# Two attention layers rewritten: halves of the array for S and T, heads of 50 stacked rows, more work on GpSimd

## The reference: two layers over a stream of 32 x 256 x 256

```
x += attn0(ln(x), ctx)   16 heads of 16, q/k/v/o projections with low-rank terms
x += sqrt((ln(x) @ cos(..))^2 + (ln(x) @ sin(..))^2)
x += attn1(ln(x), ctx)   the same heads, rotary embedding on q and k
x += quantised feed-forward, 256 -> 1024 -> 256, gelu
attn: softmax(q k^T / 4) v per head, then the output projection
```

## Time and profile before

| | us |
|---|---|
| median of 3 runs | 2490.02 (2481.99 to 2492.55) |
| span of the profiled execution | 2491.9 |
| L496 in layer 0, first to last of 32 | 124.8 to 836.1 |
| L496 in layer 1, first to last of 32 | 1093.4 to 2079.1 |

### The profile page before, as it was taken

The page is one execution under the profiler, slowest core; times in us unless marked ns, Lnnn a source line. Parts: engine busy times, 40 slices in busy tenths (PEclk is TensorE's granted clock), DMA queues, the critical chain, the costliest instruction groups (busy, mean ns, idle before and its releaser), DMA issues. The chain is left out here.

```text
span 2491.9 us, 47293 instructions
## 1 busy us (share of the span) xinstructions
PE 1955.9 (78%) x14240; PEld 1576.1 (63%) x14240; DVE 1747.3 (70%) x3674; ACT 1316.8 (53%) x2381; POOL 797.0 (32%) x866
## 2 busy tenths in 40 slices
PE   1689999999999679277788777887777775786687
PEld 0567777777777467255666666666666663665676
DVE  6567778877877378465667767767666665676788
ACT  0255666656655378144444444444444443786676
POOL 3012222222222200423333333333333332221787
PEclk9899999999999689578888888888888877898899
DMA  5576887888878100356665656666666661356565
GB/s 164 107 157 145 169 172 162 166 169 166 170 161 165 53 3 0 76 104 122 123 120 116 117 109 116 119 112 118 111 118 122 121 118 54 135 220 252 196 242 186
DMA packets 259781, 333.54 MB, mean 134 GB/s; under 512 B 29152, under 2 KB 237184, under 8 KB 251520
## 3 DMA queue, kind: packets, MB, share of 16 engines
q1 hardware_dynamic: 233088, 277.00, 49.4%
q0 software_dynamic: 26624, 55.67, 9.6%
HBM read 185.70 MB, written 144.70 MB: 133 GB/s over the span
## 5 line engine op out<-in xcount | busy, mean ns | idle before, releaser
L610 DVE TENSOR_REDUCE L_negm<-L_s_bank 128x2 f32<-128x512 f32 x1024 | 684.4, 684 | 363.2 <-PE L_s_bank L418 360.7
L475 ACT ACTIVATE L_prob<-L_t_bank 128x512 f32<-128x512 f32 x1024 | 598.9, 598 | 631.8 <-PE L_t_bank L429 625.7
L418 PE MATMUL L_s_bank<-L_kst,L_qst 96*128 96x256 f32 x2048 | 526.1, 343 | 236.5 <-DMA L_kst<-k_scratch 176.7
L418 PEld LDWEIGHTS L_s_bank<-L_kst,L_qst 96*128 96x128 f32 x2048 | 355.4, 216 | 363.0 <-issue 142.0
L429 PE MATMUL L_t_bank<-L_qst,L_kst 98*128 98x256 f32 x2048 | 460.6, 311 | 18.3 <-ACT L_prob L475 15.2
L429 PEld LDWEIGHTS L_t_bank<-L_qst,L_kst 98*128 98x128 f32 x2048 | 361.7, 217 | 33.3 <-ACT L_prob L475 30.0
L339 PE MATMUL L_o_bank<-L_prob,L_vext 128*32 128x256 f32 x4096 | 301.1, 415 | 2.7 <-ACT L_prob L475 2.7
L1289 PE MATMUL G_acc<-G_w_out,G_hhl 128*128 128x256 f32 x1024 | 140.4, 291 | 59.4 <-DVE G_hhl L1259 59.1
L259 POOL DMA_DIRECT2D L_den<-o_scratch x64 | 35.5, 554 | 452.2 <-DMA o_scratch<-L_osb 452.2
L1289 PEld LDWEIGHTS G_acc<-G_w_out,G_hhl 128*128 128x128 f32 x1024 | 127.9, 192 | 72.1 <-DVE G_hhl L1259 37.5
L339 PEld LDWEIGHTS L_o_bank<-L_prob,L_vext 128*32 128x32 f32 x4096 | 112.5, 115 | 92.6 <-issue 18.8
(11 more groups left out here) (172 smaller groups left out, 3257.2 us busy)
## 6 DMA issues: line engine op xcount, KB each, us to landing
L_qst<-q_scratch SPq DMA_DIRECT2D x384, 128.0 KB, 5.0
L_kst<-k_scratch SPq DMA_DIRECT2D x384, 128.0 KB, 6.4
q_scratch<-L_qhl SPq DMA_DIRECT2D x64, 512.0 KB, 3.0
k_scratch<-L_khl SPq DMA_DIRECT2D x64, 512.0 KB, 3.2
o_scratch<-L_osb POOLq DMA_DIRECT2D x128, 256.0 KB, 4.8
hidden_scratch<-G_hid SPq DMA_DIRECT2D x32, 1024.0 KB, 3.9
G_hid<-hidden_scratch SPq DMA_DIRECT2D x32, 1024.0 KB, 7.4
L_ctx_in<-in_ctx SPq DMA_DIRECT2D x64, 256.0 KB, 3.2
```

The costliest lines, as they stand in the source:

```text
L418: mm = pe.matmul(s_bank[k % 2][:, j, :], qst[1 - q][0:96, h, P * qt:P * (qt + 1)], kst[1 - q][0:96, h, :], start=True, stop=True)
L475: act.activation(prob[g % 2][:, k % 2, 2 * (k // 2 % 2):2 * (k // 2 % 2) + 2, :], t_bank[k % 2][:, :, :], ACT.Exp, scale=HD ** -0.5).then_ ...
L610: dve.tensor_reduce(negm[:, t, 2 * pair:2 * pair + 2, qt], s_bank[k % 2][:, :, :], AX.X, ALU.max, negate=True).then_inc(sem["dve_s"], 1)
```

## The change

- Heads are regrouped: a step at one j takes head j of either 128-row tile. Of the 8 heads of a tile, 4 sit at partitions 0 to 49 of the stacks, 4 at 64 to 113 (48 rows and 2 for maximum and ones). For batch n and half h the partitions start at 64 * (n % 2 ^ h), so that S of batch i+1 and T of batch i, issued alternately (S, T, S, T), always lie in opposite halves.
- Stacks: 8 DMAs a batch of 2 KB runs in place of 12 of 1 KB runs; no zeroed rows.
- The pipeline is one batch longer (project q and k for batch i+3), all steps written out (no `Fori`). Output products `weighted` (two a batch, 16 matmuls each, in place of four of 8) write two banks `eo` that are copied at once.
- Order on TensorE: after k = 2 maxima's transpose, project v and `weighted(i-1, 1)`; after 4 the transposes (layer 1: and project k); after 6 project q; after 7 project k (layer 0); after 10 project o, maxima's transpose and `weighted(i, 0)`.
- ScalarE takes q and k with bias as float32, v's copy, `eo`; VectorE keeps reductions, low parts of x and ctx, maxima, reciprocal, residual sum, statistics. GpSimd takes the normalisation, the splits of q and k, the low part of y, the scaling, and in layer 1 the whole rotation, whose half swap is a DMA.
- v's bias is folded into the output bias. The reciprocals are spread by a broadcasting DMA (the mask matmul goes). All DMAs go to SyncE's queue. Layer 0 stores the split transposed ctx to DRAM, and layer 1 loads it (no transposes and splits of ctx there).

The diff, cut to its core: the stacks, SyncE's step (between what stands here it issues, in order: stores of k and q, 4 DMAs; the load of ctx; sums of the exponentials, 2; half swap of k, 2, or ctx store; merge of the outputs, 4; later reciprocals out, 2; half swap of q, 2; last, reciprocals back, 1) and TensorE's step:

```diff
-        qst = [sb(f"qst{j}", [98, H, S], F32R) for j in range(2)]
+        qst = [sb(f"qst{j}", [P, HJ, KT, S], F32R) for j in range(2)]
...
+            def stack(n, half):
+                u = n % 2 ^ half
+                for st, dram, high in ((kst[n % 2], k_dram[n % 2], KH), (qst[n % 2], q_dram[n % 2], QH)):
+                    part = dram.rearrange("(j d) c t q -> j d c (t q)", d=HD)[HJ * u:HJ * (u + 1)]
+                    sp.dma_start(st[64 * u:64 * u + 2 * HD, :, :, :].bitcast(F32), part.rearrange("j d c n -> (d c) j n")).then_inc(sem[f"stack{half}"], 16)
+                    sp.dma_start(st[64 * u + 2 * HD:64 * u + ROWS, :, :, :].bitcast(F32),
+                                 part[:, :, high, :].rearrange("j d n -> d j n")).then_inc(sem[f"stack{half}"], 16)
...
+            def step(i):
+                if on(i + 1):
+                    after(sp, sem["pe_t"], 16 * i)
+                    stack(i + 1, 1)
+                if on(i):
+                    maxima(i, 1)
...
+                    after(sp, sem["pe_t"], 16 * i + 8)
+                    stack(i + 2, 0)
...
+                if on(i + 1):
+                    maxima(i + 1, 0)
...
+                for k in range(16):
+                    first = scores(i + 1, k) if on(i + 1) else iter(())
+                    second = scores_T(i, k) if on(i) else iter(())
+                    for _ in range(KT):
+                        next(first, None)
+                        next(second, None)
+                    if k == 2:
+                        if on(i):
+                            after(pe, sem["dve_mT"], 2 * i + 1)
+                            maxima(i, 1)
+                        if on(i + 2):
...
+                            project_rows(m1, cT[(i + 2) % len(cT)], whl["v"]).then_inc(sem["pe_v"], 1)
+                        if on(i - 1):
+                            weighted(i - 1, 1)
+                    if k == 4 and on(n):
...
+                    if k == 6 and on(n):
...
+                    if k == 10:
+                        if on(i - 2):
+                            pe.wait_ge(sem["pool_yl"], i - 1)
+                            after(pe, sem["act_kf"], min(n + 1, hi))
...
+                            project_rows(m1, yhl, whl["o"]).then_inc(sem["pe_o"], 1)
+                        if on(i + 1):
+                            after(pe, sem["act_qf"], min(n + 1, hi))
+                            maxima(i + 1, 0)
+                        if on(i):
+                            weighted(i, 0)
```

More of the change, by code:

```diff
@@ L197, in stack @@
[L197 to L204, removed]
@@ L433, in _, with scores @@
-            drive(pe, step)
+            def scores(n, k):
+                half, j, qt = k // 8, k % 8 // 2, k % 2
+                u = n % 2 ^ half
+                if k % 8 == 0:
+                    pe.wait_ge(sem[f"stack{half}"], 64 * (n + 1))
+                after(pe, sem["dve_s"], 16 * n + k - 1)
+                rows = slice(64 * u, 64 * u + ROWS)
+                for t in range(KT):
+                    mm = pe.matmul(s_bank[k % 2][:, t, :], qst[n % 2][rows, j, t, P * qt:P * (qt + 1)], kst[n % 2][rows, j, t, :],
+                                   start=True, stop=True)
+                    if t == KT - 1:
+                        mm.then_inc(sem["pe_s"], 1)
+                    yield
@@ new lines, in scores_T @@
+            def scores_T(n, k):
+                half, j, kt = k // 8, k % 8 // 2, k % 2
+                u = n % 2 ^ half
+                if n == lo and k == 0:
+                    pe.wait_ge(sem["ones0"], 64)
+                if k % 8 == 0:
+                    pe.wait_ge(sem[f"m_load{half}"], 16 * (n + 1))
+                after(pe, sem["act_p"], 16 * n + k - 1)
+                rows = slice(64 * u, 64 * u + ROWS + 2)
+                for t in range(KT):
+                    mm = pe.matmul(t_bank[k % 2][:, t, :], kst[n % 2][rows, j, t, P * kt:P * (kt + 1)], qst[n % 2][rows, j, t, :],
+                                   start=True, stop=True)
+                    if t == KT - 1:
+                        mm.then_inc(sem["pe_t"], 1)
+                    yield
@@ L435, in _ @@
+            drive(step)
         @block.scalar
@@ L670, in start @@
+                    if k == 13 and on(i - 2):
+                        b = i - 2 - lo
+                        dve.wait_ge(sem["dve_bn"], i - 1)
+                        for t in range(NT):
+                            ins = dve.bn_aggr(stats[:, 2 * b + t, :], bst[:, t, :])
+                        ins.then_inc(sem["dve_st"], 1)
+            drive(step)
+            dve.wait_ge(sem["dve_st"], hi)
 def start(core, x, x_res, stats, consts, src):
```

793 lines of the change are left out of this document (351 added, 442 removed).

## The result

The changed kernel takes 2748.66 us (median of 4 runs, 2741.91 to 2750.83) where the kernel before, beside it, takes 2491.28 (2481.99 to 2502.78): a ratio of 1.1033, 95% interval 1.0982 to 1.1084. The prediction was 2467, range 2320 to 2580: wrong in sign and outside the range. The profiled execution has a span of 2747.7 us at a mean granted clock of 0.803 (before: 2491.9 at 0.880).

The account below looks back on a forecast made before the run. Before, TensorE bounds layer 0, waits bound layer 1. Steps: 24.4 + 0.3 + 2.0 = 26.7 and 24.75 + 0.5 + 2.0 = 27.25; span 2491.9 + 117.8 - 141.1 = 2468.6, median 2467 us, range 2320 to 2580.

Parts of the forecast that it names:

- Halves side by side: TensorE, S and T: pairs in opposite partition halves overlap, 0.24 us for one k instead of 0.48.
- Rival C: S and T: halves do not run side by side, 0.48 a k, about 1.0 us a step; 2529 us, chance 0.10.
- The schedule of layer 0 at full clock: Layer 0's step: six parts sum to 24.4 us against 22.9 before; GpSimd beside VectorE adds 0.3.
- part 1: Layer 0, k = 11 to 2 of the next step: VectorE sets the pace, 6.35 us.
- switches of the tiling mode: TensorE: a whole matmul of 0.28 at some ten switches, 1.3 us more a step, would give 2548 us.
- The clock: Both layers: TensorE's clock falls, costing 2.0 us a step on the path; bounds nothing and 3.3.
- rival B: Blocks after k = 2 and project q: clock falls every step, 3.5 us layer 0, 2.7 layer 1; 2557 us, chance 0.20.
- ScalarE's added waits and SyncE's queue: Moved work: ScalarE has about 3 us before T 3, SyncE is 13 us of 24 busy; cost nothing.
- D: SyncE's one queue: a wait holds the stacks, S 0 waits as before; 2.2 us a step, 2603 us, chance 0.07.
- The k stack's wait of before: Layer 1: S's wait for stacks, 120.7 us for k's in the window before, goes; step 24.75 against 31.8.
- GpSimd beside VectorE: VectorE's maxima splits wait while GpSimd is busy: 0.3 us a step in layer 0, 0.5 in layer 1.
- Big blocks and VectorE's work no longer lie beside each other: Layer 0: this gives back the gain from TensorE's work dropping to some 15.8 us; step 24.4 against 22.9.

Follow-up runs that it names:

- g3: The changed kernel with S and T of one k in the same half of the array; 2872.1 us, ratio 1.152 to the kernel before.
- i3: The changed kernel with k and q stores before the second maxima, and S and T of ten k's issued twice; 2596.0 us, ratio 1.038 to the kernel before.
- g2_stores: The changed kernel with SyncE's stores of k and q ahead of the second maxima's load; 2597.2 us, ratio 1.043 to the kernel before.
- g4_spread: The changed kernel with project v moved to k = 13 and output products issued in halves at k = 1, 2, 12, 14; 2435.0 us, ratio 0.977.
- g1: The changed kernel with S and T issued twice at k = 0, 1, 3, 4, 5, 11 to 15; 2692.7 us, ratio 1.081.
- h2: The changed kernel with only v's projection moved, from after k = 2 to after k = 13 of its own batch's step; 2589.4 us, ratio 1.036.
- i1_swap_early: The changed kernel with v late, products split, stores before second maxima, and q's half swap right behind k's in SyncE's order; 2336.2 us, ratio 0.939.

## Why the prediction was wrong, step by step

1. **Halves side by side: right.** 0.24 a k, as taken. Rival C is refuted by the trace, and its price was short by half: 62 us estimated, some 120 measured. Of g3's 3.0 us a step in layer 0, half of the added low is 2.8: the price came by way of the clock.
2. **The schedule of layer 0 at full clock: near.** 24.7 with GpSimd's share; some 24.8 by i3's step at full clock. There the blocks took 3.9, 5.0 and 3.6, forecast 3.9, 4.7 and 3.65. In the change itself part 1, k = 11 to 2, was 6.35 and measured 6.3; S 3 to project q 4.7 and 4.9; the wait for k's evacuation 1.1 and 1.2. The 1.3 us that the prediction named for switches of the tiling mode is not there: these blocks leave no room for it (and ten switches of 0.28 would have been 2.8).
3. **The clock: the step that failed in layer 0.** I took 2.0 us a step, from layer 1's mean clock of before and one fall there; it costs some 5.9. The block after k = 2 took 6.8 for 3.9, project q to S 10 6.4 for 4.7, the block after k = 10 5.1 for 3.65: 6.0 more in these three, of the 6.3 by which the sum of 24.4 fell short of 30.7. My upper bound of 3.3 was itself too low: it allowed one fall a step, in the first block and project q, and there are two, and they reach project k, project o and both sets of products as well. The mechanism was rival B's, at 1.7 times its price (3.5 against 5.9): B has 28.5 us for layer 0, measured 30.7. What I had weighed wrongly was a mean: a mean clock says nothing of which work meets the low stretches, and here it is the work that everything waits for. The Trainium skill (TensorE: Matmul & The Clock Gate, Terms) puts the penalty of throttled time at half of its length; the trace comes near, 13.7 / 2 = 6.8 against the 5.9 found by parts, and 5.2 between i3's two steps.
4. **ScalarE's wait for the store: the step that failed in layer 1.** I costed ScalarE's added waits and SyncE's queue at nothing and asked only whether the stacks would be late. They were not (S waits for no DMA in either window), so D is wrong as put; but the store of q stood behind the second maxima, and g2_stores gives 5.0 us a step for it in the middle of the layer, 4.8 over all 31 distances, of which some 2.0 came through the clock. The forecast went by all distances: 27.25 + 4.8 = 32.05, of the 33.05 measured. What makes the last 1.0 isn't shown. In all: layer 0 missed by 205.2 - 117.8 = 87.4 us, layer 1 by 39.0 + 141.1 = 180.1, the rest of the program by 11.6, together the 279.1 between 2747.7 and 2468.6. The forecast took a whole step for all 31 distances; that those at the ends are shorter (29.6 against 30.7 us on average in layer 0) made the miss smaller than its terms were off.
5. **The k stack's wait of before: right**, it is gone (120.7 us to none), and without the store's wait layer 1 comes in at 28.2 over all distances (g2_stores), for 27.25.
6. **GpSimd beside VectorE: small, as said.** The split of the maxima, which answers to the earlier trace rows, in layer 0 and then in layer 1:

```profile
L559 DVE CAST L_mhl<-L_negm 128x16 fp32r<-128x16 f32 x53 | 9.3, 175 | 1.8
```

```profile
L559 DVE CAST L_mhl<-L_negm 128x16 fp32r<-128x16 f32 x53 | 24.9, 470 | 1.8
```

In layer 1 the mean is 0.3 us more, twice a step, so 0.6 in all for the cast, of which half is on the path by the schedule; in layer 0 nothing. The forecast had 0.5 and 0.3.

7. **"Big blocks and VectorE's work no longer lie beside each other": seen, and its consequence missed.** It stood in the working as the reason for 24.4 over 22.9. g4_spread shows what it was worth: 6.4 us a step, by the arithmetic of the table 1.7 in "full" and 4.7 through the clock.

## What to carry to other kernels

When a change makes part of TensorE's work cheap and gathers the rest into blocks, look at the granted clock stretch by stretch and ask which instructions meet the low ones: here the same matmuls took 30.7 or 24.4 us a step by their order alone. Every DMA issued behind a DMA that waits inherits that wait, so for each buffer that an engine overwrites, follow the queue that frees it, and after mending one such wait read the trace again for the next, which the mending itself may have made. Repeated matmuls can show that the clock is the price; spreading real work was the better cure here. And look at each step before taking a median: where long and short ones alternate, it hides the size of a gain.

## What the runs showed of the hardware

- Work added to TensorE made a step shorter: 40 redundant matmuls a step, 30.7 to 27.4 us in layer 0. The same in layer 1 (i3 against g2) made it 2.4 longer.
- The same instructions of one step took 25.75 us at full clock and 30.98 with 13.65 us of half clock (i3_stores_again, neighbouring steps).
- Busy share does not order the clocks: in 200 to 800 us TensorE was busy 530 of 600 at 0.72 (g3), 490 at 0.91 (g1), 455 at 0.92 (h2).
- How long SyncE is held by the issue of a DMA depends on more than its shape. In layer 1 of the change a q store takes 1.5 us (median of 64; 3.41 for the two shown above), in i1_swap_early the same store 0.57; a k store takes 0.6 in both. In the rows shown the slow q stores come right behind those of k; the cause was not tried. The issue of most stack loads takes 0.4 to 0.5.
- S and T in opposite halves start within 0.01 us of each other, and switching between these, full-array projections and 17-column products cost some 0.1 us or nothing: the first pair after a block takes 0.22 to the next where later ones take 0.12, and S 2 to S 3 with all of the block after k = 2 between takes 3.92 at full clock (i3_stores_again).
